# Attention in steps of two tiles, row means over DRAM, and x transposed in the last head

## The reference, cut to what matters

```
c    = mean of x over channels                       # [B, N]
diff = c[:, None, :] - c[:, :, None]
A    = ||sigmoid(diff) - 0.5| - 0.5| * 2             # symmetric
g    = relu(x^T @ (adj * A) * para)                  # [B, C, N]
q    = g as [B, heads, N, 64];  k, v = x @ kv_w
out  = softmax(q k^T * scale) v
x1   = layernorm(x + out)
```

## Time and profile before

| | |
|---|---|
| three runs, median (lowest to highest) | 3213.74 us (3212.96 to 3216.64) |
| the profiled execution's own time | 3214.61 us |
| its span, first to last instruction | 3212.8 us |
| granted TensorE clock, mean | 0.968 |
| busy: PE, DVE, ACT, POOL | 91%, 66%, 52%, 33% of the span |
| attention layer | 16 batches, g products starting from 36.9 to 2163.4 us |
| one batch in the middle | 142.1 us |

### The profile page before, as it was taken

The page is one execution under the profiler, slowest core; times in us unless marked ns, Lnnn a source line. Parts: engine busy times, 40 slices in busy tenths (PEclk is TensorE's granted clock), DMA queues, the critical chain, the costliest instruction groups (busy, mean ns, idle before and its releaser), DMA issues. The chain is left out here.

```text
span 3212.8 us, 38926 instructions
## 1 busy us (share of the span) xinstructions
PE 2929.7 (91%) x12436; PEld 1861.4 (58%) x12436; DVE 2127.5 (66%) x3015; ACT 1674.4 (52%) x1940; POOL 1066.9 (33%) x500
## 2 busy tenths in 40 slices
PE   6999999999999999999999999999779999988963
PEld 5454555555455554545455554545368888876853
DVE  6677777777677777767777776777353333337877
ACT  5465564646556464656656464654332222226768
POOL 1535344353635345263534435353420000000012
PEclk9999999999999999999999999999889999998976
DMA  4031211213021221303121121302122323226548
GB/s 132 20 119 40 78 59 59 74 44 118 25 93 55 63 65 52 99 22 114 50 68 59 59 83 35 118 26 66 50 88 92 105 79 117 78 92 216 190 157 280
DMA packets 168269, 276.13 MB, mean 86 GB/s; under 512 B 9760, under 2 KB 109088, under 8 KB 168224
## 3 DMA queue, kind: packets, MB, share of 16 engines
q1 hardware_dynamic: 168224, 275.55, 26.9%
HBM read 174.60 MB, written 67.11 MB: 75 GB/s over the span
## 5 line engine op out<-in xcount | busy, mean ns | idle before, releaser
L261 POOL TENSOR_TENSOR psum<-psum,probs 128x1024 f32<-128x1024 f32 x320 | 820.5, 2564 | 213.4 <-ACT probs L326 203.9
L326 ACT ACTIVATE probs<-sc_ps 128x1024 f32<-128x1024 f32 x512 | 523.3, 1024 | 648.7 <-PE sc_ps L793 648.1
L504 DVE TENSOR_REDUCE mx<-mx_ps 128x1 f32<-128x512 f32 x768 | 492.9, 684 | 168.0 <-PE mx_ps L761 162.1
L809 PE MATMUL pv_ps<-probs,v 128*64 128x512 f32 x2048 | 549.9, 615 | 2.8 <-ACT probs L326 2.6
L793 PE MATMUL sc_ps<-qa,ka 128*128 128x512 f32 x1024 | 441.1, 439 | 0.0
L793 PE MATMUL sc_ps<-qb,kb 128*128 128x512 f32 x1024 | 401.6, 397 | 0.0
L261 POOL TENSOR_TENSOR psum<-probs 128x1024 f32<-128x1024 f32 x64 | 152.7, 2386 | 695.3 <-ACT probs L326 378.0
L793 PEld LDWEIGHTS sc_ps<-qa,ka 128*128 128x128 f32 x1024 | 195.9, 193 | 260.8 <-issue 140.4
L761 PE MATMUL mx_ps<-ka,qa 128*128 128x512 f32 x768 | 299.2, 442 | 18.0 <-DVE xT_lo L458 6.4
L761 PEld LDWEIGHTS mx_ps<-ka,qa 128*128 128x128 f32 x768 | 135.3, 188 | 220.8 <-DVE mx L504 140.5
L723 PE MATMUL sc_ps<-w_hi,x_hi 128*128 128x512 f32 x512 | 211.0, 412 | 44.1 <-DVE w_lo L471 44.1
(11 more groups left out here) (182 smaller groups left out, 5285.1 us busy)
## 6 DMA issues: line engine op xcount, KB each, us to landing
adj_ring<-in_adj_dram SPq DMA_DIRECT2D x128, 512.0 KB, 3.8
pre_scratch<-pre SPq DMA_DIRECT2D x32, 1024.0 KB, 4.2
hid<-pre_scratch SPq DMA_DIRECT2D x32, 1024.0 KB, 5.0
x<-in_x_dram SPq DMA_DIRECT2D x16, 1024.0 KB, 7.4
kb<-ka SPq DMA_DIRECT2D x64, 256.0 KB, 3.1
qa<-qa SPq DMA_DIRECT2D x64, 256.0 KB, 3.3
res<-in_x_dram SPq DMA_DIRECT2D x16, 1024.0 KB, 5.6
x_scratch<-res SPq DMA_DIRECT2D x16, 1024.0 KB, 4.3
```

The costliest lines, as they stand in the source:

```text
L261: pool.tensor_tensor(psum[:, :], probs[:, 0, :] if k == 1 else psum[:, :], probs[:, k % PR, :], ALU.add).then_inc(s["pool_added"], 1)
L326: nc.scalar.activation(probs[:, i % PR, :], sc_ps[:, t % 2, :], ACT.Exp, scale=SCALE)\
L504: nc.vector.tensor_reduce(mx2[:, nh, n:n + 1], mx_ps[:, nh, :], AX.X, ALU.max)\
L809: ins = nc.tensor.matmul(pv_ps[nh * HD:(nh + 1) * HD, h % 2, :], v[:, i, h * HD:(h + 1) * HD], probs[:, i % PR, nh * BANK:(nh + 1) * BANK] ...
```

## The change

- **Pairs.** Heads run in four steps of two tiles. Both tiles' scores are issued, then `values` of the two tiles of the step before, one after the other. At a head's start the step ends with the last two `values` of the head before and its `sum_up`; the two tiles' part 0 is issued ahead of both parts 1. `sum_up` writes the other half of `pv_ps`.
- **Buffers.** `psum` has two buffers: the first addition of a head waits for `sum_up` of two heads before instead of one; `probs` has four instead of three; `kb` two instead of four, so copies of heads 2 and 3 are later.
- **Means.** `broadcast_means`, `sum_channels` and `mean_columns` are gone. `x_high` is eight instructions of 256 which also give the row sums (`accum_out=csum`), in head 1. SyncE writes the sums to DRAM, waits, and reads them back into `cb` on all partitions (`spread_sums`). Nodes are laid out as (p t) instead of (t p) for this.
- **Placement.** Both `transpose_x` are in head 3; `distance` and `tanh_half` of tiles 0 to 2 in head 2; `weigh(0)` and `weigh(1)` on VectorE at the end of head 2, `split_x` at the end of head 1; `q_low(2)` and `q_low(3)` one at the start of head 1 and one of head 2.

```diff
-    WR, DR, AR, PR = 3, 3, 2, 3
+    WR, DR, AR, PR = 3, 3, 2, 4
+    MAX_FIRST = [0, 1, 1, 1]
+    MAX_MID = [0, 1, 1, 0]
+    MAX_LAST = [1, 1, 1, 0]
+    DEN_PAIR, BACK_PAIR = 1, 2
-        psum = sb("psum", [P, N])
+        psum = sb("psum", [P, 2, N])
...
+            def spread_sums(b):
+                wait(sp, s["xhi_done"], T * (b + 1))
+                sp.dma_start(sums_v, csum[:, :]).then_inc(s["sums_out"], 16)
+                wait(sp, s["sums_out"], 16 * (b + 1))
+                wait(sp, s["abs_done"], 8 * b)
+                sp.dma_start(cb[:, :], sums_row).then_inc(s["cb_in"], 16)
...
-                for h in range(1, HEADS):
-                    store_row(b, h)
+                store_row(b, 1)
+                copy_kb(b, 2)
                 if not last:
+                    spread_sums(b + 1)
+                store_row(b, 2)
+                copy_kb(b, 3)
+                if not last:
+                    load_adj(b + 1, 2)
+                store_row(b, 3)
+                if not last:
+                    load_adj(b + 1, 3)
                     copy_kb(b + 1, 0)
...
-                            wait(pool, s["sum_ready"], 4 * b + h)
+                            wait(pool, s["sum_ready"], 4 * b + h - 1)
...
+                for n in tiles:
+                    nc.scalar.activation(x_hi[:, n, :], x32[:, n, :], ACT.Copy, accum_out=csum[:, n:n + 1])\
+                        .then_inc(s["xhi_done"], 1)
+
+            def prepare(b, h, p):
+                if h == 1 and p < 3:
+                    x_high(b, (range(0, 2), range(2, 5), range(5, 8))[p])
+                if h == 2 and p:
+                    distance(b, p - 1)
+                    tanh_half(b, p - 1)
+                if (h, p) == (3, 0):
                     xt_high(b, 0)
+                if (h, p) == (3, 1):
+                    w_high(b, 0)
                     xt_high(b, 1)
                     w_high(b, 1)
+                if (h, p) == (3, 2):
+                    w_high(b, 2)
                     distance(b, 3)
                     tanh_half(b, 3)
+                    k_high(b, 0)
+                    k_high(b, 1)
...
                 for h in (1, 2):
                     add_last(b, h - 1)
-                    maxima(b, h + 1, range(0, 3))
+                    q_low(b, h + 1)
+                    maxima(b, h + 1, range(0, 4))
...
                     maxima_row(b, h + 1)
+                    if h == 1 and not last:
+                        split_x(b + 1)
                     if h == 2 and not last:
-                        sum_channels(b + 1)
-                        mean_columns(b + 1)
-                        split_x(b + 1)
+                        weigh(b + 1, 0)
+                        weigh(b + 1, 1)
...
+                        if h and p == BACK_PAIR:
+                            transpose_back(b, h - 1)
+                        maxes(MAX_FIRST[p])
+                        if p == 0:
+                            for part in (0, 1) if h else (1,):
+                                scores(b, h, i, [part])
+                                scores(b, h, i + 1, [part])
+                        else:
+                            scores(b, h, i)
+                            maxes(MAX_MID[p])
+                            scores(b, h, i + 1)
+                        maxes(MAX_LAST[p])
+                        if h and p == DEN_PAIR:
+                            transpose_sums(b, h - 1)
+                        if more and p == PAIRS - 1:
                             transpose_maxima(b, h + 1)
                         if not last:
+                            prepare(b + 1, h, p)
+                        if p:
+                            values(b, h, i - 2)
+                            values(b, h, i - 1)
+                        elif h:
+                            values(b, h - 1, T - 2)
+                            values(b, h - 1, T - 1)
                             sum_up(b, h - 1)
```

More of the change, by code:

```diff
@@ L3 @@
 from contextlib import ExitStack
+import itertools
 F32 = mybir.dt.float32
@@ L181, in body @@
             def body(b, last):
+                load_adj(b, 4)
                 if not last:
                     load_x(b + 1)
-                for n in range(4, T):
+                for n in range(5, T):
                     load_adj(b, n)
@@ L391, in body @@
                     head_copy(b - 1, HEADS - 1)
[L392 to L398 removed]
+                distance(b, 4)
+                tanh_half(b, 4)
+                w_high(b, 3)
+                if before:
+                    den_copy(b - 1, HEADS - 1)
+                distance(b, 5)
+                tanh_half(b, 5)
+                w_high(b, 4)
+                distance(b, 6)
+                tanh_half(b, 6)
+                w_high(b, 5)
+                distance(b, 7)
+                tanh_half(b, 7)
+                w_high(b, 6)
+                w_high(b, 7)
                 q_high(b, 0)
@@ L615, in body @@
                     k_low(b + 1, 0)
                     k_low(b + 1, 1)
-                    w_low(b + 1, 0)
-                    weigh(b + 1, 2)
-                    w_low(b + 1, 1)
-                    weigh(b + 1, 3)
-                    w_low(b + 1, 2)
+            split_x(0)
+            for n in range(3):
+                weigh(0, n)
             xt_low(0, 0)
+            w_low(0, 0)
             xt_low(0, 1)
-            sum_channels(0)
-            mean_columns(0)
-            for n in range(2):
-                weigh(0, n)
+            w_low(0, 1)
@@ L752, in max_scores @@
                         wait(pe, s["v_evac"], 2 * b + 2)
-                    elif not last:
-                        wait(pe, s["xtl_done"], 2 * b + h + 1)
                 for nh in range(NH):
@@ L870, in body, with maxes @@
                 for h in range(HEADS):
-                    n = 0
                     more = h + 1 < HEADS
-                    for i in range(T):
-                        scores(b, h, i, [1] if h == 0 and i < 2 else (0, 1))
-                        if more and MAX_BEFORE[i]:
-                            max_scores(b, h + 1, n, last)
-                            n += 1
-                        if more and i == ROW_STEP:
+                    tiles = iter(range(T))
+                    def maxes(count):
+                        for n in itertools.islice(tiles, count if more else 0):
+                            max_scores(b, h + 1, n)
```

265 lines of the change are left out of this document (100 added, 165 removed).

## The result

The changed kernel takes 3174.0 us (median of 4 runs, 3170.9 to 3178.7), the kernel before 3213.6 (median of 4): a ratio of 0.9876 (95% interval 0.9859 to 0.9893). It is faster by 1.2%, 40 us, where 90 were forecast. The profiled execution took 3170.9 us with a span of 3169.1, so the two spans differ by 43.7 us.

A forecast was written before the change was run, and what follows sets the result against it. TensorE's own work plus its waits bound the kernel. Per batch -5.8 - 1.85 - 4.5 + 3.5 + 0.75 + 1.5 = -6.4; fifteen give -96, the last -5.8, clock +12: -90 against 3214.6, so 3124 us, range 3045 to 3185.

The forecast's parts named there:

- clock: Matmuls behind a stall may run at the lower clock level; taken for half the batches, 12 us in all (0 to 25).
- head 2's wait: In head 2, q_low(3) held by GpSimd's addition or a late row 2 stalls TensorE: 1.5 us a batch (0.2 to 3.5).
- Pairs: Pairing values blocks cuts groups per batch from 32 to 16, at 0.36 us each: 5.8 us a batch saved.
- Means: The eight matmuls for the means go from TensorE: 1.85 us a batch saved.
- Waits that go: Waits for xT_lo (0.43) and, in the g product, psum and w_lo (4.1) end: 4.5 us a batch (0 to 4.5).
- Row 3: At head 3's start TensorE waits for the row, queued behind a load that waits for weigh(0): 3.5 us a batch.
- Head 1: At head 1's start part 1 waits for q_low(1), held by GpSimd's addition: 0.75 us a batch (0 to 0.8).
- At nothing: Costs counted as zero: x_high in eight pieces, later kb copies, three max_scores with only scores between, transpose_x in head 3.
- the new waits hardly show: Rival, chance 0.2: row 3 costs 1.1 us, head 2 0.2, no clock loss; -10.9 a batch, 3046 us.
- The round trip costs more: Rival, chance 0.2: means' trip through DRAM makes row 2 4 us late, clock falls every batch; -3.1 a batch, 3162 us.

The follow-up runs named there:

- e1_row3: The changed kernel with head 3's row stored ahead of load_adj(b+1, 2) in SyncE's queue: 3076.0 us.
- e3_filler: The changed kernel with 14 unneeded matmuls of 512 columns between part 0 and part 1 of head 3's first scores, the row wait kept: 3143.9 us.
- e2_qlow3: The changed kernel with q_low(3) made in head 1, right behind q_low(2), instead of in head 2: 3120.2 us.
- e6_psum: e4_both with GpSimd's first addition of a head waiting for the sum_up of the head before, as with one buffer of row sums: 3023.0 us.
- e4_both: The changed kernel with the edits of e1_row3 and e2_qlow3 together: 3022.5 us.
- e7_vsplit_qlow1: e4_both with one v tile ahead of the transpose of head 0's maxima and q_low(1) right behind q_low(0): 3008.8 us.

## Why the prediction was wrong, point by point

The direction and the mechanisms held; the size did not, 40 us where 90 were forecast. The step that failed is the term of the **clock**: "A stall of 3.5 us may do this. I take half the batches, 12 us in all (0 to 25)." It happens in every batch and behind both stalls: 2.6 us in head 3 (e1_row3; 2.5 by e3_filler) and 1.75 in head 2 (e2_qlow3), 4.35 x 15 = 65 us. I had read the price in the earlier trace rows, eight matmuls at 0.42, from a short stretch, and not asked what longer waits would bring, nor allowed any for head 2. Those rows are also no general price of the g product's waits: they come from the sixth batch, and of the sixteen g products of the kernel before it is the only one with a granted clock of 0.5. The kernel before has such stretches too, most of them about the end of the stage of the maxima, and I did not credit the change with ending them, but they cost little: a middle batch of it without any takes 141.6 us, the mean one 142.1.

The second is **head 2's wait**: "I take 1.5 (0.2 to 3.5)". It measured 2.94. My own two branches were 0.2 and 2.6, and I took the middle of a thing that had only two outcomes. That is 1.4 x 15 = 22 us. The way into it was another than I wrote: `x_lo` was not held by the addition, it held the addition; either way `q_low(3)` met the next one.

The rest, step by step:

- **Pairs**: right in kind, 0.39 to 0.42 a group instead of 0.36, so 0.5 to 1 us a batch more than the 5.8. The last batch agrees in size. Of its 11 us, 4.8 are the g product's; the 6.2 that are left, and its two small new waits (0.8 and 0.5), make 7.5 where sixteen groups give 6.2 to 6.7.
- **Means**: the eight matmuls are gone. The sums landed 1.4 us and `cb` 3.6 us after their issue (medians), 5.0 together where the prediction's estimate was 5.2. The section that the estimate cites gives its figure for DMAs that GpSimd issues; these are SyncE's.
- **Waits that go**: all three went, 4.5 us. The g product went from 28.9 to 24.1 us, as forecast ("some 5 us"), 0.7 more than its two waits. The reason I gave for `psum` fell with e6_psum.
- **Row 3**: 4.2 for 3.5, because the store behind a load of `adj` needed 3.15 us to land and not 1.86 to 2.86. Issued ahead of the load in e1_row3 (at 677.71), it held up nothing at 680.19, 2.5 us later. SyncE's issue order and the held `weigh(0)` were as written. 10 us.
- **Head 1**: 0.79 for 0.75.
- **At nothing**: the `max_scores` behind head 0's first part wait 0.6 us a batch, 9 us. The reads of the accumulator, the later copies and `cb` showed nowhere as a wait of TensorE. `row` 2 was not late.

By the forecast the fifth batch should have changed by -5.6 (with the clock's 0.8). It changed by -2.5. The known differences are +3.55 clock, -0.5 for the low stretches before, +1.4 head 2, +0.7 row 3, +0.6 maxima, -0.7 pairs and -0.7 g product. That makes -1.25, so 1.25 us a batch of further gain stay unassigned. The last batch has about 1 us of it too, though no work for a next batch runs there. In head 2 the change without its wait and its low stretch (21.7 against 26.5) is about 1.4 more than means and pairs explain; its cause was not tested.

Of the rivals, "the new waits hardly show" names what the edits could have been worth: 3046 us by its terms, 3022 measured once both waits are taken out (e4_both). "The round trip costs more" put the clock in every batch, which was right, for a reason that was not: row 2 was on time. Its sum is wrong too. It adds 0.8 for the clock, but the clock in every batch is 1.6 by the prediction's own price; with 1.6 it gives -2.3 a batch and 3174 us. That this is the measured time is luck. The recorded range holds 3174 only because its upper end was taken from this rival; the forecast's own range ended at 3155.

## What to carry to other kernels

A wait of several microseconds on TensorE has a second price: what runs behind it may run at half the clock, here 1.75 to 2.6 us on top of waits of 2.9 and 4.2, so a new stall in every iteration is to be costed with it, in every iteration. A transfer that TensorE needs soon does not belong behind an issue that waits for VectorE: one moved line in SyncE's queue was worth 98 us, more than twice the whole change. And where a cost has two outcomes, take the likelier and put the other in the range: the 1.5 us taken for head 2 lay between two outcomes and was neither.

## What the runs showed of the hardware

- The granted clock shows two levels here, 1.0 and 0.5 (2.4 and 1.2 GHz), and in the middle batches the low stretches are 3.4 or 6.8 us long. One can begin within a wait (704.68, the wait ends at 706.05) or after it (684.20, with the wait over at 682.51).
- The same wait does not always bring it. The 2.0 us for `mxs` in the stage of the maxima is the same in the changed kernel (16.28 us with clock 1.00 in the fifth batch, 17.48 us with 0.91 in the sixth, and so on in turn) and in e4_both (17.48 us, 0.91 in each middle batch); cutting it in two brought 1.00 in all but a few batches (e7_vsplit_qlow1). Work that nobody needs removed a low stretch of 6.8 us and made the kernel 30 us faster.
- Where GpSimd's addition and an instruction of VectorE with two SBUF inputs meet, either can be the one that stands still: `weigh` and `q_low` lost about 2 us behind an addition, and an addition took 4.58 us behind `x_lo`. The Trainium skill (SBUF — State Buffer, SBUF: two separate sides) places contention of the engines on the port that these two share; the trace agrees, in both directions. It does not show that the first to start wins: by the profile that addition began 0.07 us ahead of `x_lo`, and starts on GpSimd are rough.
- A store of one `row` landed 3.15 us after its issue behind a 512 KB load issued 0.4 us before it, and 1.9 where no load of `adj` stood ahead of it.
